# Splitting the output products of six of eight attention units into three rounded products

## The chip, the cores and the metric

One core of a Trainium2 chip. The time is the device time of the one core, in microseconds (us). An instruction queue each for TensorE (PE; its weight loads are shown as PEld), VectorE (DVE), ScalarE (ACT), GpSimd (POOL) and SyncE (SP, which here only starts transfers); each queue works strictly in order, and the queues wait for one another through semaphores.

## The reference, cut to what matters

Four batches of 512 rows of 128 numbers go through a layer norm, an attention with 16 heads of 64 and one shared key and value head, a projection back, a second norm, and a mixture of eight experts with two chosen per row:

```python
xn = _layernorm(x, ln1_g, ln1_b)
q = xn @ Wq;  k, v = split(xn @ Wkv)
attn = softmax((q * SCALE) @ k.T)
out = attn @ v                                   # 16 heads side by side: 1024 wide
x = x + _layernorm(out @ Wo, ln2_g, ln2_b)
gu = x_normed @ gate_up_w.T                      # for each expert, rows routed to it
x = x + combine(down_w @ (up * gelu(gate)))
```

The change is about `out @ Wo`. It is computed transposed: for each of the 8 pairs of heads of a batch (k counts them over all batches, 0 to 31) a 128x128 piece of Wo times the pair's 128x512 normalised attention output, summed over the 8 pairs in one bank of PSUM, `y_ps`.

## The kernel before, in words

**Units and slots.** The attention runs over 8 units, each half of a batch: 8 heads, that is 4 pairs. `attention_schedule` (L28 to L96) writes the order of all work by hand: a unit has 32 slots, one for each block of 128 keys of a head, and every step has a slot and, within it, a rank. All five engines walk the same sorted list of steps and do their own part of each. In a slot TensorE computes one 128x512 block of scores (EXP: two matmuls, L1298 and L1300, with operands rounded to fp32r), and one block for the row maxima of a later head (MAX, L1278, one matmul of fp32r); ScalarE takes the exponential (L1203), VectorE the maximum (L1123). In 4 of each 8 slots TensorE also multiplies probabilities and values (PV, L1314, in fp32). After each head (every fourth slot) GpSimd adds up its probabilities in two instructions (`fold` L1049, `psums` L1055), and for each pair it copies q (`q_hm`, L1029). Steps SUM, SUMS, SPREAD, RECIP, GATHER make the reciprocals of the softmax sums.

**Normalising and projecting a pair.** Unit u is normalised and projected while unit u+1 runs; this text calls the 32 slots of unit n stretch n, so stretch 4 holds the work on the pairs of unit 3. For pair c of a unit (0 to 3):
- NORM: TensorE spreads the reciprocals over a bank (`sum_ps`, L861, one fp32r matmul) once the pair before has been multiplied; VectorE multiplies into `ao`, which has two slots, taken in turn (L795).
- OUT: TensorE multiplies the piece of Wo (`wof`) with `ao` in fp32 (L871). A matmul of fp32 is two records in the trace.
- NORM of pair k waits, on VectorE, until OUT of pair k-2 has read its slot of `ao` (L794).

NORM stands in slots 14, 17, 19 and 22, OUT five slots later. The steps that a batch's second norm, its routing (CHOOSE0 to CHOOSE7, RANK, PLACE) and the tile lists (LIST0 to LIST3) need are spread over later slots (`AFTER_AT`). The routed rows of the first two batches leave by eight indirect transfers that GpSimd itself starts (SEND, L497), one every second slot from slot 5 to slot 19 of stretches 4 and 6. In stretches 2 and 4 a batch's input is prepared as well: XT (slot 17), XL on GpSimd (slot 17, L1059), K on TensorE (slot 21), which waits for XL. VectorE's MAX for the last head is in slot 9 of stretch 7, so TensorE waits for no maximum after that.

**The expert weights.** `raw_w` (128 partitions x 8 experts x 1024) lies in memory of its own and is filled by eight transfers at the V step of the last batch (L973 to L976, slot 25 of stretch 4). They are first used after the attention.

**The end of the attention.** In stretch 7 VectorE makes the routing and the list of the third batch, and sums the last head itself (L1144); SUM waits for it. The expert part follows in a second block of code.

Of the kernel before, what the change touches and what calls it, by code (L numbers as in the profile page):

```python
# [5 lines left out]
F32 = mybir.dt.float32  # L6
F32R = mybir.dt.float32r
# [5 lines left out]
P = 128  # L13
# [14 lines left out]
def attention_schedule(units):  # L28

    slots, lead = UH * JT, MAX_LEAD
    placed = []

    def place(slot, order, kind, u, a):
        placed.append((slot, order, (kind, u, a)))

    for n, kind in enumerate(IN_STEPS):

        place(FIRST_V_AT if kind in ("V", "VC") else -1000 + n, 4, kind, 0, 0)
        for b in range(1, units // 2):

            place(2 * slots * (b - 1) + IN_AT[n] + (LATER if b == 1 else 0), 4, kind, b, 0)
    for b in range(units // 2 - 1):
        at, lag = (AFTER_AT, 2) if b < units // 2 - 2 else (LATE_AFTER_AT, 0.25)
        for n, kind in enumerate(AFTER_STEPS):
            place(2 * slots * (b + 1) + at[n], 4, kind, b, 0)  # L60
        for n in range(TOP_K * JT if b < units // 2 - 2 else EARLY_SENDS):
            place(2 * slots * (b + 1) + at[AFTER_STEPS.index("PLACE")] + lag * n, 4.5, "SEND", b, n)
    for pair in range(units * UP):
        u, p = divmod(pair, UP)

        at = (-30, -11, *FIRST_Q_AT)[pair] if pair < 4 else 8 * pair - 19 - lead
        place(at, 3, "Q", u, p)
        place(at + 1, 3, "QHI", u, p)

        place(-8 if pair == 1 else at + 1, 4, "QLO", u, p)  # L70
        for jt in range(JT):
            place(8 * pair + PV_AT[jt], 2, "PV", u, p * JT + jt)
        place(8 * pair + PV_AT[-1] + 1, 1, "RAW", u, p)
    for n in range(units * slots):
        u, a = divmod(n, slots)
        place(n, 0, "EXP", u, a)
        place(n - 15 if n < 12 else (n - 12) // 2 if n < 32 else n - 16 - lead, 1, "MAX", u, a)
    for n, (head, _) in enumerate(shifts(units)):
        place(FIRST_SHIFT_AT[n] if n < 2 else JT * head - lead + 1, 3, "SHIFT", n, 0)
    for u in range(units):  # L80
        after = slots * (u + 1)
        if u < units - 1:
            place(after + SUM_AT[0], 5, "SUM", u, 0)
            place(after + SUM_AT[1], 5, "SUM", u, 1)
            for n, kind in enumerate(RECIP_STEPS):
                place(after + RECIP_AT[n], 5, kind, u, 0)
            for c in range(UP):
                place(after + NORM_AT[c], 5, "NORM", u, c)
                place(after + NORM_AT[c] + OUT_LAG, 5, "OUT", u, c)
        else:  # L90
# [17 lines left out]

PV_AT = (6, 8, 9, 11)

NORM_AT = (14, 17, 19, 22)

OUT_LAG = 5

RECIP_STEPS = ("SUMS", "SPREAD", "RECIP", "GATHER")

# [62 lines left out]
def bass_preln_mqa_moe_kernel(nc, x, ln1_g, ln1_b, wq, wkv, wo, ln2_g, ln2_b, gate_wT, gate_upT, downT,  # L179
# [32 lines left out]
    with ExitStack() as whole:  # L212
        def sb(stack, name, shape, dt=F32):
            return stack.enter_context(nc.sbuf_tensor(name, shape, dt))
# [4 lines left out]
        def sem(name):  # L219
            return whole.enter_context(nc.semaphore(name))  # L220
# [54 lines left out]
        jumps = sb(whole, "jumps", [P, 2 * E])  # L275
        second = sb(whole, "second", [P, REST])

        raw_w = sb(whole, "raw_w", [P, E * 2 * F])
        xs_early = sb(whole, "xs_early", [P, EARLY_ROWS, ROW])

        psums = sb(whole, "psums", [P, SUM_SLOTS, S])
# [466 lines left out]
        def load_rows(sp, k, dst):  # L748
# [6 lines left out]
            x_turned xnT_sb xh_ready xl_ready k_mm kh_ready kl_ready v_mm v_ready  # L755
            q_mm q_hi q_lo q_top max_mm max_done mrow_ready score_mm exp_done
            pv_mm raw_ready prob_folded head_sum sum_mm recip_done norm_mm ao_ready
            out_mm sums_copied spread_in rhl_in hs_in""".split()
        (wkv_in, wq_in, wo_in, ones_set, wkv_split, wq_split, headsel_set,
         x_turned, xnT_sb, xh_ready, xl_ready, k_mm, kh_ready, kl_ready, v_mm, v_ready,  # L760
         q_mm, q_hi, q_lo, q_top, max_mm, max_done, mrow_ready, score_mm, exp_done,
         pv_mm, raw_ready, prob_folded, head_sum, sum_mm, recip_done, norm_mm, ao_ready,
         out_mm, sums_copied, spread_in, rhl_in, hs_in) = [sem(n) for n in names]
        def vector_sums(head):


# [12 lines left out]
        def tail_vector(dve, kind, u, a):  # L779
            if kind == "RECIP":  # L780
                dve.wait_ge(spread_in, 32 * (u + 1))
                link(dve, nc.vector.reciprocal(rinv[:, :], spread[:, :]))
                if u >= 1:
                    dve.wait_ge(rhl_in, 32 * u)
                link(dve, nc.vector.tensor_copy(halves[:, 0, :], rinv[:, :]))
                nc.vector.tensor_tensor(halves[:, 1, :], rinv[:, :], halves[:, 0, :].bitcast(F32),
                                        ALU.subtract).then_inc(recip_done, 1)
            if kind == "NORM":
                k = u * UP + a
                dve.wait_ge(norm_mm, k + 1)  # L790
                dve.wait_ge(raw_ready, k + 1)

                if k >= 2:
                    dve.wait_ge(out_mm, k - 1)  # L794
                nc.vector.tensor_tensor(ao[:, k % 2, :], sum_ps[:, :], raw[:, k % RAW_SLOTS, :],  # L795
                                        ALU.mult).then_inc(ao_ready, 1)

# [19 lines left out]
        def tail_scalar(act, kind, u, a):  # L817
            if kind == "SUMS":
                act.wait_ge(sum_mm, 2 * (u + 1))
                if u >= 1:  # L820
                    act.wait_ge(spread_in, 32 * u)
                nc.scalar.activation(sums[:, :], sum_ps[:, :], ACT.Copy).then_inc(sums_copied, 1)
            if kind == "RAW":
                k = u * UP + a
                act.wait_ge(pv_mm, k + 1)
                if k >= RAW_SLOTS:

                    act.wait_ge(ao_ready, k - RAW_SLOTS + 1)
                nc.scalar.activation(raw[:, k % RAW_SLOTS, :], pv_ps[:, :], ACT.Copy).then_inc(raw_ready, 1)
            if kind == "OUT" and (u * UP + a) % PAIRS == PAIRS - 1:  # L830
                b = (u * UP + a) // PAIRS
                act.wait_ge(out_mm, PAIRS * (b + 1))
                if b >= 1:

                    act.wait_ge(y_turned, b)
                if b >= 1:

                    act.wait_ge(logit_mm, b)
                nc.scalar.activation(yT[:, :], y_ps[:, :], ACT.Copy).then_inc(y_ready, 1)

        def tail_tensor(pe, kind, u, a):

            b = u // 2
            if kind == "SUM":
# [18 lines left out]
            if kind == "OUT":  # L863
                k = u * UP + a
                c = k % PAIRS
                pe.wait_ge(ao_ready, k + 1)
                if k == 0:
                    pe.wait_ge(wo_in, 16)
                if c == 0 and b >= 1:
                    pe.wait_ge(y_ready, b)  # L870
                nc.tensor.matmul(y_ps[:, :], wof[:, c, :], ao[:, k % 2, :], start=c == 0,  # L871
                                 stop=c == PAIRS - 1).then_inc(out_mm, 1)


        last_pv = max(n for n, step in enumerate(steps) if step[0] == "PV")
        tail_steps = [step for step in steps[last_pv:] if step[0] in ("RAW", *RECIP_STEPS, "NORM", "OUT")]
        assert all(step in tail_steps or step[0] in ("PV", "SUM") for step in steps[last_pv:])
        steps = [step for step in steps if step not in tail_steps]

        with ExitStack() as att:  # L880
            q_hl = sb(att, "q_hl", [P, Q_SLOTS, S], F32R)
            q_hm = sb(att, "q_hm", [P, Q_SLOTS, S], F32R)
            xh = sb(att, "xh", [P, 2, S], F32R)
# [48 lines left out]
            def _(sp):  # L932
# [20 lines left out]
                for kind, u, a in steps:  # L953
# [18 lines left out]
                                         blank[:, :, :]).then_inc(rows_filled, 16)  # L972
                    if kind == "V" and u == NB - 1:  # L973
                        sp.wait_ge(rows_filled, 16 * FILLS)
                        for e in range(E):
                            load_gate_up(sp, e)  # L976
                sp.wait_ge(tiles_ready, 1)
                sp.wait_ge(rows_sent, 16 * TOP_K * TPB * (LB - 1))
# [4 lines left out]
            def _(pool):  # L983
# [27 lines left out]
                for kind, u, a in steps:  # L1011
# [29 lines left out]
                    if kind == "EXP" and a % JT == JT - 1:  # L1041
                        head = u * UH + a // JT
                        if not vector_sums(head):
# [8 lines left out]
                            if head >= SUM_SLOTS:  # L1052

                                pool.wait_ge(sum_mm, (head - SUM_SLOTS) // 4 + 1)
                            nc.gpsimd.tensor_tensor(psums[:, head % SUM_SLOTS, :], fold[:, 0, :], fold[:, 1, :],  # L1055
                                                    ALU.add).then_inc(head_sum, 1)
                    if kind == "XL" and u >= 1:
                        pool.wait_ge(xh_ready, u + 1)
                        nc.gpsimd.tensor_tensor(xl[:, u % 2, :], xnT[:, :], xh[:, u % 2, :].bitcast(F32),  # L1059
                                                ALU.subtract).then_inc(xl_ready, 1)  # L1060
# [149 lines left out]
            def _(pe):  # L1210
# [23 lines left out]
                for kind, u, a in steps:  # L1234
# [84 lines left out]
                    if (kind, u, a) == ("SUM", last_unit, 1):  # L1319

                        pe.wait_ge(tiles_ready, 1)
                        for k in range(OPEN):
                            load_expert(pe, k)
                    tail_tensor(pe, kind, u, a)
                    if kind in AFTER_STEPS:
                        after_tensor(pe, kind, u, q_ps)

# [1 line left out]
        with ExitStack() as moe:  # L1329


            GU, DN = 2 * F, FC * P
            wh = sb(moe, "wh", [P, E * GU], F32R)
            wl = sb(moe, "wl", [P, E * GU], F32R)
            wd = sb(moe, "wd", [P, E * DN])
# [494 lines left out]
```

## Time and profile before

| | |
|---|---|
| three runs | 603.86, 604.21 and 606.01 us, median 604.21 |
| profiled execution, its own time | 605.66 us |
| its span, first to last instruction | 603.7 us |
| busy: PE, PEld, DVE, ACT, POOL | 571.4, 326.3, 399.3, 297.8, 393.8 us |
| granted TensorE clock, mean | 0.983 |
| OUT of pairs 0 to 23 in the trace | 111.5 us (first) to 398.2 us (last) |

A row of the timeline gives start, duration, engine, line, operation and tiles, how many records were merged, and in brackets how long the engine had been idle and what released it. Matmuls are pipelined: the duration of one is longer than its turn, which is read from one start to the next.

### The profile page before, as it was taken

How to read it: one execution, taken by the hardware profiler on the slowest of the kernel's cores; microseconds unless marked ns; L12 is line 12 of the kernel's file. 1: busy time of each engine (PE TensorE's matmuls, PEld its weight loads, DVE VectorE, ACT ScalarE, POOL GpSimd, SP SyncE). 2: the span in 40 equal slices, each digit the busy share in tenths (PEclk: the TensorE clock that was granted, in tenths of full speed). 3: DMA queues.
4: the chain of work that ended last, by engine and by line, in shares of the span. 5: the costliest groups of instructions: out<-in, count | busy, mean ns of one | idle time of the engine just before them, and what ended most of it. 6: DMA issues, size and time to landing. Idle time of an engine off the chain costs nothing. (4 is left out here: it accounts for less than half of the span.)

```text
span 603.7 us, 8807 instructions
## 1 busy us (share of the span) xinstructions
PE 571.4 (95%) x2543; PEld 326.3 (54%) x2543; DVE 399.3 (66%) x875; ACT 297.8 (49%) x559; POOL 393.8 (65%) x329
## 2 busy tenths in 40 slices
PE   8799999999999999998999999899998898899992
PEld 6464455444545554444545545444443577788882
DVE  4878656657756869774567777876485458444463
ACT  3235655545636564463556445355635564355541
POOL 6448776667758866798598568949745944345332
PEclk9889999999999999998999999999998999999997
DMA  5111012010201200062000000000004410231042
GB/s 167 71 72 71 2 71 75 0 73 1 75 1 72 74 2 1 7 233 81 1 3 2 1 1 25 16 2 3 11 0 119 119 31 23 58 91 47 19 141 89
DMA packets 27805, 29.46 MB, mean 49 GB/s; under 512 B 7763, under 2 KB 19285, under 8 KB 27760
## 3 DMA queue, kind: packets, MB, share of 16 engines
q1 hardware_dynamic: 25056, 24.27, 12.5%
q0 software_dynamic: 2272, 4.24, 2.1%
q8 instruction: 23, 0.38, 0.3%
q10 hardware_dynamic: 432, 0.39, 0.2%
q14 instruction: 22, 0.18, 0.1%
HBM read 13.50 MB, written 15.32 MB: 48 GB/s over the span
## 5 line engine op out<-in xcount | busy, mean ns | idle before, releaser
L1203 ACT ACTIVATE prob<-s_ps 128x512 f32<-128x512 f32 x256 | 150.8, 599 | 183.3 <-PE s_ps L1300 180.9
L1123 DVE TENSOR_REDUCE less_max<-max_ps 128x1 fp32r<-128x512 f32 x256 | 174.0, 689 | 81.0 <-PE max_ps L1278 78.6
L1049 POOL TENSOR_TENSOR fold<-prob 128x1024 f32<-128x1024 f32 x63 | 149.6, 2375 | 88.7 <-ACT prob L1203 88.0
L1314 PE MATMUL pv_ps<-prob,v 128*64 128x512 f32 x512 | 138.5, 621 | 0.0
L1298 PE MATMUL s_ps<-q_hl,khh 128*128 128x512 f32 x256 | 117.9, 460 | 0.7 <-ACT prob L1203 0.7
L1278 PE MATMUL max_ps<-khh,q_hl 128*128 128x512 f32 x256 | 103.0, 408 | 5.4 <-DVE less_max L1123 4.8
L1300 PE MATMUL s_ps<-q_hm,kly 65*128 65x512 f32 x256 | 101.9, 398 | 0.0
L1298 PEld LDWEIGHTS s_ps<-q_hl,khh 128*128 128x128 f32 x256 | 48.6, 190 | 85.8 <-ACT prob L1203 67.1
L1055 POOL TENSOR_TENSOR psums<-fold 128x512 f32<-128x512 f32 x63 | 80.8, 1282 | 4.9
L1278 PEld LDWEIGHTS max_ps<-khh,q_hl 128*128 128x128 f32 x256 | 49.1, 192 | 23.4 <-DVE less_max L1123 11.1
L1300 PEld LDWEIGHTS s_ps<-q_hm,kly 65*128 65x128 f32 x256 | 48.8, 191 | 9.2 <-issue 3.3
L1314 PEld LDWEIGHTS pv_ps<-prob,v 128*64 128x64 f32 x512 | 25.6, 135 | 46.2 <-issue 34.3
L497 POOL DMA_INDIRECT sorted_rows<-xr,place_i x32 | 33.9, 1059 | 22.7 <-issue 10.9
L1108 DVE TENSOR_TENSOR q_hl<-q_ps,q_hl 64x512 fp32r<-64x512 f32 x64 | 44.1, 689 | 6.3 <-ACT q_hl L1185 4.9
L1531 DVE TENSOR_TENSOR ha<-up_ps,gl 128x512 f32<-128x512 f32 x39 | 26.9, 690 | 29.3 <-PE up_ps L1668 21.7
L1185 ACT ACTIVATE q_hl<-q_ps 64x512 fp32r<-64x512 f32 x64 | 37.6, 587 | 12.4 <-PE q_ps L1215 11.5
L1492 POOL DMA_INDIRECT parts<-raw,psums x22 | 21.8, 992 | 29.5 <-DVE raw L1540 24.3
L795 DVE TENSOR_TENSOR ao<-sum_ps,raw 128x512 f32<-128x512 f32 x32 | 22.1, 690 | 27.5 <-PE sum_ps L861 27.4
L1029 POOL TENSOR_SCALAR q_hm<-q_hl 64x1024 fp32r<-64x1024 f32 x32 | 33.3, 1041 | 8.0 <-ACT q_hl L1185 8.0
L871 PE MATMUL y_ps<-ao,wof 128*128 128x512 f32 x64 | 35.9, 646 | 0.0
L1605 ACT ACTIVATE ht<-q_ps 128x512 f32<-128x512 f32 x39 | 23.3, 597 | 23.5 <-PE q_ps L1677 23.5
L1690 PE MATMUL sum_ps<-wd,ht 128*128 x216 | 29.1, 278 | 4.6 <-DVE raw L1540 3.2
(252 smaller groups left out, 772.0 us busy)
## 6 DMA issues: line engine op xcount, KB each, us to landing
sorted_rows<-raw_w SPq DMA_DIRECT2D x36, 260.0 KB, 2.6
raw_w<-in_gate_upT SPq DMA_DIRECT2D x8, 512.0 KB, 8.5
wd<-in_downT SPq DMA_DIRECT2D x8, 256.0 KB, 4.1
raw_w<-parts SPq DMA_DIRECT2D x6, 256.0 KB, 3.4
psums<-sorted_rows SPq DMA_DIRECT2D x22, 65.0 KB, 1.9
x<-in_x SPq DMA_DIRECT2D x4, 256.0 KB, 4.2
xs_first<-sorted_rows SPq DMA_DIRECT2D x15, 65.0 KB, 1.8
out<-x SPq DMA_DIRECT2D x3, 256.0 KB, 2.1
```

The lines of the kernel that those rows point to most:

```text
L497: nc.gpsimd.indirect_dma_start(out=sorted_rows, out_offset=bass.IndirectOffsetOnAxis(ap=place_i[:, n, t:t + 1], axis=0), in_=xr[:, n, t, : ...
L871: nc.tensor.matmul(y_ps[:, :], wof[:, c, :], ao[:, k % 2, :], start=c == 0, stop=c == PAIRS - 1).then_inc(out_mm, 1)
L1049: nc.gpsimd.tensor_tensor(fold[:, :, :], prob[:, head % 4, 0:2, :], prob[:, head % 4, 2:4, :], ALU.add).then_inc(prob_folded, 1)
L1055: nc.gpsimd.tensor_tensor(psums[:, head % SUM_SLOTS, :], fold[:, 0, :], fold[:, 1, :], ALU.add).then_inc(head_sum, 1)
L1108: nc.vector.tensor_tensor(q_hl[DH:P, h % Q_SLOTS, :], q_ps[DH * hd:DH * hd + DH, :], q_hl[0:DH, h % Q_SLOTS, :].bitcast(F32), ALU.subtract ...
L1123: nc.vector.tensor_reduce(less_max[:, group % 2, col:col + 1], max_ps[:, k % 2, :], AX_X, ALU.max, negate=True).then_inc(max_done, 1)
L1185: nc.scalar.activation(q_hl[0:DH, (2 * k + hd) % Q_SLOTS, :], q_ps[DH * hd:DH * hd + DH, :], ACT.Copy).then_inc(q_hi, 1)
L1203: nc.scalar.activation(prob[:, head % 4, jt, :], s_ps[:, k % 2, :], ACT.Exp, scale=SCALE).then_inc(exp_done, 1)
L1278: nc.tensor.matmul(max_ps[:, k % 2, :], q_hl[:, k // JT % Q_SLOTS, it * P:(it + 1) * P], khh[:, b % 2, :], start=True, stop=True).then_inc ...
L1298: nc.tensor.matmul(s_ps[:, k % 2, :], khh[:, b % 2, keys], q_hl[:, slot, :], start=True, stop=False)
L1300: nc.tensor.matmul(s_ps[:, k % 2, :], kly[0:DH + 1, b % 2, keys], q_hm[0:DH + 1, slot, :], start=False, stop=True).then_inc(score_mm, 1)
L1314: last = nc.tensor.matmul(pv_ps[DH * hd:DH * hd + DH, :], v[:, b % 2, jt, :], prob[:, head % 4, jt, :], start=(jt == 0), stop=(jt == JT - 1))
```

## The change: what it does

For pairs 0 to 23 (units 0 to 5) OUT becomes three fp32r matmuls: high part of Wo times high part of `ao`, low times high, high times low. ScalarE makes the high part of `ao` (new step HIGH), GpSimd subtracts for the low part (LOW); both go to `hl`, which has three slots. GpSimd also splits Wo once, one 128x128 piece after each of heads 2 to 9. NORM moves to slots 14, 16, 19, 21, OUT to 21, 23, 25, 27, for all units but the last. NORM of pair k now waits for LOW of pair k-2 where that pair is split, for its OUT otherwise. `woh` and `hl` lie where the weights of experts 4 to 7 go; those four transfers are started after OUT of pair 23. Pairs 24 to 31 keep the fp32 product.

```diff
             for c in range(UP):
                 place(after + NORM_AT[c], 5, "NORM", u, c)
-                place(after + NORM_AT[c] + OUT_LAG, 5, "OUT", u, c)
+                if u < SPLIT_UNITS:
+                    place(after + HIGH_AT[c], 5, "HIGH", u, c)
+                    place(after + LOW_AT[c], 5, "LOW", u, c)
+                place(after + OUT_AT[c], 5, "OUT", u, c)
...
-NORM_AT = (14, 17, 19, 22)
-
-OUT_LAG = 5
+NORM_AT = (14, 16, 19, 21)
+
+HIGH_AT = (15, 17, 20, 22)
+
+LOW_AT = (18, 18, 22, 22)
+
+OUT_AT = (21, 23, 25, 27)
+
+HL_SLOTS = 3
+
+FIRST_WEIGHTS = 4
+
+SPLIT_UNITS = 6
...
-        raw_w = sb(whole, "raw_w", [P, E * 2 * F])
+        GU = 2 * F
+        with ExitStack() as split_units:
+
+            sb(split_units, "first_weights", [P, FIRST_WEIGHTS * GU])
+            woh = sb(split_units, "woh", [P, PAIRS, P], F32R)
+            hl = sb(split_units, "hl", [P, 2, HL_SLOTS, S], F32R)
+        raw_w = sb(whole, "raw_w", [P, E * GU])
...
                 if k >= 2:
-                    dve.wait_ge(out_mm, k - 1)
+                    if k - 2 < SPLIT_UNITS * UP:
+                        dve.wait_ge(al_ready, k - 1)
+                    else:
+                        dve.wait_ge(out_mm, k - 1)
                 nc.vector.tensor_tensor(ao[:, k % 2, :], sum_ps[:, :], raw[:, k % RAW_SLOTS, :],
                                         ALU.mult).then_inc(ao_ready, 1)
...
+            if kind == "HIGH":
+                k = u * UP + a
+                act.wait_ge(ao_ready, k + 1)
+
+                if k >= HL_SLOTS:
+                    act.wait_ge(out_mm, k - HL_SLOTS + 1)
+                nc.scalar.activation(hl[:, 0, k % HL_SLOTS, :], ao[:, k % 2, :],
+                                     ACT.Copy).then_inc(ah_ready, 1)
...
-                pe.wait_ge(ao_ready, k + 1)
...
-                nc.tensor.matmul(y_ps[:, :], wof[:, c, :], ao[:, k % 2, :], start=c == 0,
-                                 stop=c == PAIRS - 1).then_inc(out_mm, 1)
+                slot = k % HL_SLOTS
+                if u >= SPLIT_UNITS:
+                    pe.wait_ge(ao_ready, k + 1)
+                    nc.tensor.matmul(y_ps[:, :], wof[:, c, :], ao[:, k % 2, :], start=c == 0,
+                                     stop=c == PAIRS - 1).then_inc(out_mm, 1)
+                else:
+                    pe.wait_ge(wo_split, min(k, PAIRS - 1) + 1)
+                    pe.wait_ge(ah_ready, k + 1)
+                    nc.tensor.matmul(y_ps[:, :], woh[:, c, :], hl[:, 0, slot, :], start=c == 0, stop=False)
+                    nc.tensor.matmul(y_ps[:, :], wol[:, c, :], hl[:, 0, slot, :], start=False, stop=False)
+                    pe.wait_ge(al_ready, k + 1)
+                    nc.tensor.matmul(y_ps[:, :], woh[:, c, :], hl[:, 1, slot, :], start=False,
+                                     stop=c == PAIRS - 1).then_inc(out_mm, 1)
...
-                        for e in range(E):
+                        for e in range(FIRST_WEIGHTS):
+                            load_gate_up(sp, e)
+                    if (kind, u, a) == ("OUT", SPLIT_UNITS - 1, UP - 1):
+
+                        sp.wait_ge(out_mm, SPLIT_UNITS * UP)
+                        for e in range(FIRST_WEIGHTS, E):
                             load_gate_up(sp, e)
...
+                        if 2 <= head < 2 + PAIRS:
+
+                            if head == 2:
+                                pool.wait_ge(wo_in, 16)
+                            part = head - 2
+                            link_pool(pool, nc.gpsimd.tensor_scalar(woh[:, part, :], wof[:, part, :], 1.0, 1.0, ALU.mult,
+                                                                    ALU.mult))
+                            nc.gpsimd.tensor_tensor(wol[:, part, :], wof[:, part, :], woh[:, part, :].bitcast(F32),
+                                                    ALU.subtract).then_inc(wo_split, 1)
+                    if kind == "LOW":
+                        k = u * UP + a
+                        slot = k % HL_SLOTS
+                        if k >= HL_SLOTS:
+                            pool.wait_ge(out_mm, k - HL_SLOTS + 1)
+                        pool.wait_ge(ao_ready, k + 1)
+                        pool.wait_ge(ah_ready, k + 1)
+                        nc.gpsimd.tensor_tensor(hl[:, 1, slot, :], ao[:, k % 2, :], hl[:, 0, slot, :].bitcast(F32),
+                                                ALU.subtract).then_inc(al_ready, 1)
```

## Rows read from the trace of the kernel before

**Rows 1.** The page's groups: busy us, mean ns of one, idle before, releaser.
```profile
L1203 ACT ACTIVATE prob<-s_ps 128x512 f32<-128x512 f32 x256 | 150.8, 599 | 183.3 <-PE s_ps L1300 180.9
L1049 POOL TENSOR_TENSOR fold<-prob 128x1024 f32<-128x1024 f32 x63 | 149.6, 2375 | 88.7 <-ACT prob L1203 88.0
```
**Rows 2.** Windows by stretch: PE, PEld, DVE, ACT, POOL busy, clock, DMA share, GB/s.
```profile
102.00:153.00 51.00, 51.00 (x202) 24.56 (x200) 33.67 (x64) 24.98 (x46) 34.73 (x25) 1.00 0.12 44
...
260.00:317.00 57.00, 55.37 (x222) 27.34 (x221) 34.79 (x65) 29.52 (x58) 47.31 (x35) 0.97 0.23 84
...
371.00:423.00 52.00, 50.39 (x199) 23.63 (x197) 38.88 (x84) 26.19 (x50) 42.27 (x33) 1.00 0.03 9
```
**Rows 3.** Timeline of PE, stretch 1: PV, OUT, NORM, scores; then a rounded product.
```profile
114.90 1.08 PE L1314 MATMUL pv_ps<-prob,v 128*64 128x512 f32 x4
115.91 1.12 PE L871 MATMUL y_ps<-ao,wof 128*128 128x512 f32 x2
116.47 0.79 PE L861 MATMUL sum_ps<-rhl,headsel 128*128 128x512 f32 x1
117.10 0.39 PE L1298 MATMUL s_ps<-q_hl,khh 128*128 128x512 f32 x1
...
117.80 0.40 PE L1213 MATMUL q_ps<-xh,wqh 128*128 128x512 f32 x1
...
118.50 0.39 PE L1298 MATMUL s_ps<-q_hl,khh 128*128 128x512 f32 x1
```
**Rows 4.** The same of stretch 3: PV and NORM with no OUT between them.
```profile
212.79 1.08 PE L1314 MATMUL pv_ps<-prob,v 128*64 128x512 f32 x4
...
213.80 0.50 PE L861 MATMUL sum_ps<-rhl,headsel 128*128 128x512 f32 x1
214.14 0.40 PE L1298 MATMUL s_ps<-q_hl,khh 128*128 128x512 f32 x1
```
**Rows 5.** Windows of POOL alone: length, busy, instructions; between and in the SEND stretches.
```profile
253.90:281.00 27.10, 25.00 (x19) 0.94 0.49 174
370.40:392.50 22.10, 20.64 (x15) 1.00 0.06 19
220.00:253.90 33.90, 19.58 (x16) 1.00 0.01 1
```
**Rows 6.** Timeline of stretch 4, slots 19 to 23.
```profile
271.05 0.79 PE L861 MATMUL sum_ps<-rhl,headsel 128*128 128x512 f32 x1
...
273.45 1.27 POOL L1059 TENSOR_TENSOR xl<-z,xh 128x512 fp32r<-128x512 f32 x1
...
274.87 0.47 PE L1213 MATMUL q_ps<-xh,wkh 128*128 128x512 f32 x1 [1.63 <-POOL xl L1059]
274.89 0.99 POOL L497 DMA_INDIRECT sorted_rows<-xr,place_i  x1 [0.17 <-issue]
...
276.61 1.97 PE L1314 MATMUL pv_ps<-prob,v 128*64 128x512 f32 x4
```
**Rows 7.** Timeline of stretch 6, slots 19 to 23.
```profile
381.19 1.12 PE L871 MATMUL y_ps<-ao,wof 128*128 128x512 f32 x2
...
383.02 0.97 POOL L497 DMA_INDIRECT sorted_rows<-xr,place_i  x1 [0.30 <-issue]
...
384.21 2.28 DVE L655 TENSOR_TENSOR cmp<-more,tri 128x64 f32<-128x64 f32 x1
...
388.21 1.29 DVE L1123 TENSOR_REDUCE less_max<-max_ps 128x1 fp32r<-128x512 f32 x2
...
388.95 0.50 PE L1278 MATMUL max_ps<-khh,q_hl 128*128 128x512 f32 x1 [1.53 <-DVE less_max L1123]
```
**Rows 8.** Timeline of stretch 7: the unsplit pairs, and the end of the attention.
```profile
432.80 1.13 PE L871 MATMUL y_ps<-ao,wof 128*128 128x512 f32 x2
...
434.25 0.69 DVE L795 TENSOR_TENSOR ao<-sum_ps,raw 128x512 f32<-128x512 f32 x1 [1.42 <-PE sum_ps L861]
...
444.19 0.22 DVE L655 TENSOR_TENSOR cmp<-more,tri 128x64 f32<-128x64 f32 x1
...
455.33 1.06 PE L851 MATMUL sum_ps<-psums,sumsel 128*32 128x512 f32 x8 [1.37 <-DVE psums L1144]
```
**Rows 9.** Timeline of POOL at the start: splitting a 128x256 piece of another weight.
```profile
10.30 0.41 POOL L990 TENSOR_SCALAR wqh<-prob 128x256 fp32r<-128x256 f32 x1
10.79 1.09 POOL L991 TENSOR_TENSOR wql<-prob,wqh 128x256 fp32r<-128x256 f32 x1
```

More of the change, by code:

```diff
@@ L276, in bass_preln_mqa_moe_kernel @@
         second = sb(whole, "second", [P, REST])
-        raw_w = sb(whole, "raw_w", [P, E * 2 * F])
+        GU = 2 * F
[4 more added lines that the diff above has]
+        raw_w = sb(whole, "raw_w", [P, E * GU])
+        assert PAIRS * P + 2 * HL_SLOTS * S == (E - FIRST_WEIGHTS) * GU
         xs_early = sb(whole, "xs_early", [P, EARLY_ROWS, ROW])
@@ L757, in bass_preln_mqa_moe_kernel @@
             pv_mm raw_ready prob_folded head_sum sum_mm recip_done norm_mm ao_ready
-            out_mm sums_copied spread_in rhl_in hs_in""".split()
+            out_mm sums_copied spread_in rhl_in hs_in ah_ready al_ready wo_split""".split()
         (wkv_in, wq_in, wo_in, ones_set, wkv_split, wq_split, headsel_set,
@@ L762, in bass_preln_mqa_moe_kernel @@
          pv_mm, raw_ready, prob_folded, head_sum, sum_mm, recip_done, norm_mm, ao_ready,
-         out_mm, sums_copied, spread_in, rhl_in, hs_in) = [sem(n) for n in names]
+         out_mm, sums_copied, spread_in, rhl_in, hs_in, ah_ready, al_ready, wo_split) = [sem(n) for n in names]
         def vector_sums(head):
@@ L839, in tail_scalar, with tail_tensor @@
                 nc.scalar.activation(yT[:, :], y_ps[:, :], ACT.Copy).then_inc(y_ready, 1)
-        def tail_tensor(pe, kind, u, a):
+        def tail_tensor(pe, kind, u, a, wol=None):
             b = u // 2
@@ L870, in tail_tensor @@
                     pe.wait_ge(y_ready, b)
-                nc.tensor.matmul(y_ps[:, :], wof[:, c, :], ao[:, k % 2, :], start=c == 0,
-                                 stop=c == PAIRS - 1).then_inc(out_mm, 1)
+                slot = k % HL_SLOTS
[11 more added lines that the diff above has]
+                                     stop=c == PAIRS - 1).then_inc(out_mm, 1)
         last_pv = max(n for n, step in enumerate(steps) if step[0] == "PV")
-        tail_steps = [step for step in steps[last_pv:] if step[0] in ("RAW", *RECIP_STEPS, "NORM", "OUT")]
+        tail_steps = [step for step in steps[last_pv:] if step[0] in ("RAW", *RECIP_STEPS, "NORM", "HIGH", "LOW", "OUT")]
         assert all(step in tail_steps or step[0] in ("PV", "SUM") for step in steps[last_pv:])
@@ L880, in bass_preln_mqa_moe_kernel @@
         with ExitStack() as att:
+            wol = sb(att, "wol", [P, PAIRS, P], F32R)
             q_hl = sb(att, "q_hl", [P, Q_SLOTS, S], F32R)
@@ L1323, in _ @@
                             load_expert(pe, k)
-                    tail_tensor(pe, kind, u, a)
+                    tail_tensor(pe, kind, u, a, wol)
                     if kind in AFTER_STEPS:
@@ L1329, in bass_preln_mqa_moe_kernel @@
         with ExitStack() as moe:
-            GU, DN = 2 * F, FC * P
+            DN = FC * P
             wh = sb(moe, "wh", [P, E * GU], F32R)
```

## The prediction

> **What bounds the kernel now.** I read the windows by stretch first. In stretch 1 TensorE is busy for all 51.00 us of 51.00, in stretch 4 for 55.37 of 57.00, in stretch 6 for 50.39 of 52.00, while ScalarE and VectorE have a quarter or more of each stretch free and GpSimd is at 34.73 of 51, 47.31 of 57 and 42.27 of 52 us [rows 2]. So through the attention every instruction taken from TensorE shortens the run by its turn, and every wait of TensorE lengthens it. The page's groups say the same: the exponentials and the folds had 183.3 and 88.7 us of idle time ahead of them, nearly all spent on what TensorE drives [rows 1].
>
> Then I looked at GpSimd alone, because it has the highest load beside TensorE. In the middle of stretch 4 it is busy 25.00 of 27.10 us, in stretch 6 20.64 of 22.10, but only 19.58 of 33.90 between [rows 5]. What is missing in the first two windows are gaps of some 0.2 to 0.3 us around the indirect transfers (0.17 and 0.30 in the rows), so there GpSimd has no time left. Both places show in TensorE: K waits 1.63 us for GpSimd's XL, and behind that wait the PV group at 276.61 takes 1.97 us where another takes 1.08: the mean granted clock of that window is 0.94, so a few us of it ran at the lower level, 1.2 GHz [rows 3, 5, 6]. In stretch 6 a MAX waits 1.53 us for VectorE, whose list step has an instruction of 2.28 us beside a fold, where the same one takes 0.22 us in stretch 7 [rows 7, 8].
>
> **What goes, on TensorE.** With OUT between PV and NORM, from the start of PV to the scores after it are 117.10 - 114.90 = 2.20 us; with NORM alone 214.14 - 212.79 = 1.35 us. One OUT in fp32 costs 0.85 us [rows 3, 4]. A rounded product of three fp32r matmuls takes 118.50 - 117.80 = 0.70 us [rows 3], the same shapes and type as the new one. That is 0.15 to 0.16 us less for each of 24, **3.8 us** in all, and the most this change can give through TensorE. Its bounds: 24 x 0.34 = 8 us if the three overlapped so well that each cost 0.17, to a loss of 24 x (3 x 0.34 - 0.85) = 4 us if each of them came as slowly as the scores behind a fp32 product (214.14 - 213.80 = 0.34 us) [rows 4]; I take 0.70, since its own row shows it.
> The Trainium skill (FP8 and Floating Point Precision, section TensorE Precision Notes) says that true FP32 is four passes through the array. By that alone three passes would save a quarter of 0.85, 0.21 us each or 5.1 us. The trace speaks for 3.8.
>
> **What is added and hidden.** HIGH is a 128x512 activation, 0.60 us as the exponentials [rows 1]: 24 of them, 14.4 us, on an engine idle for half of each stretch. I cost them at nothing: HIGH of the first pair runs right behind its exponential, in the gap before the next scores are there. If that cover were gone each would push an exponential by up to 0.6 us, which TensorE notices only two blocks later. Splitting Wo is 8 pieces of at most half the 128x256 pair of 0.41 and 1.09 us, so up to 8 x 1.5 = 12 us even unhalved, over 50 us in which GpSimd is idle for a third: nothing on the path [rows 2, 9]. On SP the four late transfers stand behind OUT of pair 23, near 399 us; their first reader comes only behind the last SUM of the attention at 455.33 [rows 8], when TensorE waits for all eight, so over 50 us of delay cost nothing. The earlier four leave the queue sooner; as nothing waited for them, no gain.
>
> **LOW is what is not hidden.** It is a GpSimd subtraction of 128x512, as XL is: 1.27 us [rows 6]. Four per stretch are 5.1 us. In stretch 1 GpSimd has 16 us free, and 14 in the 33.9 us before the transfers of stretch 4 [rows 2, 5]; stretches 1, 2, 3 and 5 have no such transfers, and there I take it that LOW of pair 0 is done by the time that NORM of pair 2 wants its slot of `ao`. From the order of steps, NORM of pair 2 (slot 19) now waits on VectorE for LOW of pair 0 (slot 18); behind it queue all later maxima, and on TensorE OUT of pair 0 and NORM of pair 3 (slot 21) wait for the same LOW. TensorE's NORM of pair 2 takes the place where OUT stood. TensorE has two blocks (2 x 0.70) and OUT ahead of NORM of pair 3; VectorE needs 0.7 us for its multiplication and about 0.1 for the handing over. So LOW may end up to 1.5 us after NORM of pair 2 starts. This is the point from which it decides.
> - Stretch 4. GpSimd ends XL at 274.72 and the transfer of slot 17 at 275.88, so LOW ends at 277.2. NORM of pair 2 starts at about 270.6, the start of OUT before. LOW is 5 us past the point. TensorE waits for XL at K as before (now from 272.2), ends K at 275.6, waits in OUT to 277.3 and in NORM to 278.0, then maxima and the low part of k run late on VectorE. By counting turns the scores of slot 24 start at 282.9, and did at 281.6 before; as two cheaper OUTs (0.3 us) are in this, the wait costs 1.6 us. The lower clock cost some 1.4 us before (1.97 - 1.08 for PV, as much relatively for OUT behind it); with twice the idle time I take one more such piece, 1.5 us. **+3.1 us**, with bounds of 0 (all absorbed) and 5.
> - Stretch 6. The transfer of slot 17 ends at 383.99, LOW at 385.3, against 381.3 for NORM of pair 2 [rows 7]. VectorE's multiplication ends at 386.1. Only then does it take the next maximum and LIST0, which took 4.3 us (383.9 to 388.2), because two of its instructions sat out a fold and a sum; the fold is pushed back by the two LOWs and meets it again. Its next maximum ends at 391.6, so the MAX on TensorE that started at 388.95 starts at 391.7. Before it OUT of pair 1 was already done, now it comes after: +0.7. The scores of slot 24 start 3.5 us later; without the two savings inside, **+3.8 us**. Bounds 1 (the list step meets no fold) and 7 (two pieces at the lower clock).
> - Stretch 7. Pair 26 may not overwrite `ao` until OUT of pair 24 has read it, and that OUT has moved from slot 19 (before NORM) to 21 (behind it). So VectorE waits for two score blocks and an OUT: 2 x 0.47 + 0.1 + 0.85 us from NORM on, and NORM of pair 27 on TensorE waits 0.8 for the multiplication behind it. Slots 21 and 23 have no PV beside them, so each fp32 OUT there costs a change of type and back, 0.2 us. VectorE's list chain is as late, and TensorE's last SUM waits for it already (1.37 us) [rows 8]. **+1.6 us**, bounds 0.5 and 3.
>
> Sum: -3.8 + 3.1 + 3.8 + 1.6 = **+4.7 us**. The profiled execution took 605.66 us, 1.96 over its span; it would be 610.4. It lies 1.45 over the median of the runs, so against the median of 604.21 the forecast is **608.8 us**.
>
> **Rivals.**
> 1. *LOW is there in time* (not slower). If VectorE's wait costs nothing, because GpSimd reaches LOW within 1.5 us of NORM, the gain of 3.8 stays and only stretch 7 pays: 604.2 - 3.8 + 1.6 = 602.0, or 600.4 if that is hidden too. For it: a third of GpSimd's time in stretch 1 is idle. Against it: in stretches 4 and 6 it is the order of its own queue, not speed elsewhere, that puts LOW behind two transfers, and these windows have none to give.
> 2. *The waits are half as long*: TensorE meets them with work that I have put after them, or the lower clock stays away. Stretches 4 and 6 then cost 3.3 together: 604.2 - 3.8 + 3.3 + 1.6 = 605.3.
> 3. *VectorE becomes the bound by the shared memory path.* The 2.28 us against 0.22 shows that a small VectorE instruction can sit out a GpSimd one. Routing steps of stretches 3 and 5 and lists of 6 and 7 stand in slots 20 to 31, next to LOW. Four more MAX waits of 1.5 us like that of stretch 6 make 608.8 + 6 = 615. Against: in stretches 3 and 5 LOW ends before the routing's instructions with two memory operands begin. The Trainium skill (SBUF — State Buffer, section SBUF: two separate sides) says that GpSimd and a VectorE instruction with two SBUF inputs take the pair of ports as a lock for the whole instruction. By it the maxima and multiplications, which read PSUM, don't suffer, and each LOW may hold up a list instruction.
> 4. *Change without effect*: the weights' memory or Wo's split could stall the start; no row has anything waiting there.
>
> **How the numbers follow.** About 0.5%, 3.0 us, can be told from no change. Forecast 0.52, own range 607.2 to 611.5. Rival 1 0.13: half of it below 601.2. Rival 2 with rival 4 0.25, between 603 and 607. Rival 3 0.10, above 611.5. So faster 0.07, same 0.31 (0.06 + 0.25), slower 0.62. The range leaves out the faster tail and half of rival 3: 602.0 to 612.5.
>
> **What would show it.** Right: PE waits named after VectorE's multiplication or LOW in stretches 4 and 6, LOW of pair 12 ending some 5 us after NORM of pair 14 starts; a later `ao` multiplication of pair 26 than of the OUT of 24; stretches 1, 2, 3 and 5 shorter by about 0.6 us each. Wrong: GpSimd taking LOW before the transfers, or TensorE's stretches 4 and 6 as long as before. A clock below 0.983 over the span would say that the lower level cost more than I took.

## The result, and the profile after

The changed kernel takes 612.00 us (median of 4 runs, 611.81 to 612.21), the kernel before, on the same chip, 604.04 us (603.81 to 606.01): ratio 1.0125, 95% interval 1.0104 to 1.0147. It is slower by 8.0 us. The forecast was 608.8 us and slower; the direction is right, the size is 3.2 us short. The measured time lies inside the stated range of 602.0 to 612.5 us but 0.5 us above the narrower range given to the mechanism forecast, 607.2 to 611.5.

The profiled execution of the changed kernel took 611.81 us, 609.7 of it span, at a mean clock of 0.978 (before: 605.66, 603.7 and 0.983). From its page: the load of the engines, and the two groups of [rows 1] as they are now.

```profile
PE 572.4 (94%) x2567; PEld 330.6 (54%) x2567; DVE 398.4 (65%) x875; ACT 311.6 (51%) x583; POOL 430.3 (71%) x369
L1268 ACT ACTIVATE prob<-s_ps 128x512 f32<-128x512 f32 x256 | 151.1, 599 | 161.8 <-PE s_ps L1365 158.4
L1096 POOL TENSOR_TENSOR fold<-prob 128x1024 f32<-128x1024 f32 x63 | 149.9, 2380 | 56.4 <-ACT prob L1268 55.6
```

GpSimd has 36.5 us more work (430.3 against 393.8) and ScalarE 13.8; the folds still cost 150 us but have 32 us less free time ahead of them. TensorE's busy time rose by a microsecond although 24 products became cheaper; some 27 us of its span ran at the lower clock, some 20 in the first profile of before.

The windows of [rows 2] again. Their bounds are not those of the stretches: in the trace before, stretch 1 runs from 79.9 to 132.4 us, stretch 4 from 239.3 to 297.4, stretch 6 from 350.3 to 404.3, so each window goes from about slot 14 of its stretch to slot 14 of the next. In the first of them TensorE is still never idle, in the other two its busy time fell (55.37 to 53.39, and 50.39 to 49.07 us) and the granted clock with it (0.97 to 0.94, and 1.00 to 0.97).

```profile
102.00:153.00 51.00, 51.00 (x207) 25.48 (x208) 34.00 (x65) 27.71 (x52) 40.16 (x29) 1.00 0.12 44
...
260.00:317.00 57.00, 53.39 (x216) 27.50 (x214) 31.41 (x58) 29.79 (x58) 49.77 (x37) 0.94 0.14 45
...
371.00:423.00 52.00, 49.07 (x193) 24.00 (x191) 37.61 (x78) 27.03 (x50) 44.09 (x34) 0.97 0.15 51
```

To say where the time went I took, from both traces, the start of the score block at a given slot, counted from the first score block of the attention. "1.00" is slot 0 of stretch 1; a number is the kernel named minus the first profile of before, in us (negative: ahead). "End" is the end of the last instruction. The other columns are kernels described below. Four of them (e1, e6, e7, e8) had no spell at half clock between 30 and 35 us, where the other six profiles had one, and are 0.8 to 0.9 us ahead in every line from there on; e8 is the kernel before itself, so this is no effect of a change in the code.

```
slot        after    e1     e2     e3     e4     e5     e6     e7     e8
0.08         0.0   -0.9   +0.1    0.0    0.0    0.0   -0.8   -0.9   -0.8
2.00        -0.5   -1.3    0.0   -0.5   -0.5   -0.5   -1.5   -1.5   -0.8
4.00        -1.2   -2.0    0.0   -1.2   -1.2   -1.1   -2.5   -2.5   -0.8
4.16        -1.2   -2.0    0.0   -1.2   -1.1   -1.1   -2.5   -2.5   -0.8
4.24        +2.3   -5.8   -3.4   +2.4   +0.7   -2.7   -6.2   -6.2   -2.4
6.16        +1.9   -5.9   -3.4   +1.9   +0.3   -2.8   -6.6   -6.7   -2.3
6.24        +5.0   -6.4   -5.2   +5.1   +3.1   -2.8   -7.0   -7.2   -2.4
7.00        +4.8   -6.5   -5.2   +5.0   +2.9   -2.8   -7.4   -6.2   -2.4
7.16        +4.8   -5.4   -4.2   +5.0   +2.9   -2.8   -6.2   -6.2   -2.4
last SUM    +5.9   -4.3   -3.1   +5.0   +4.0   -2.8   -5.1   -5.2   -2.3
end         +6.2   -0.7   -2.2   +7.9   +5.3   -2.0   -3.8   -3.4   -0.2
```

In column "after", stretches 1, 2, 3 and 5 gain 0.45, 0.56, 0.19 and 0.16 us; stretch 4 loses 3.3, stretch 6 3.0, stretch 7 1.1, the expert part 0.3.

The timeline of stretch 4 shows how. It answers to [rows 6].

```profile
270.98 1.07 POOL L517 DMA_INDIRECT sorted_rows<-xr,place_i  x1 [0.17 <-issue]
272.08 1.27 POOL L1124 TENSOR_TENSOR xl<-z,xh 128x512 fp32r<-128x512 f32 x1
273.49 0.47 PE L1278 MATMUL q_ps<-xh,wkh 128*128 128x512 f32 x1 [2.52 <-POOL xl L1124]
273.51 0.99 POOL L517 DMA_INDIRECT sorted_rows<-xr,place_i  x1 [0.17 <-issue]
274.53 2.51 POOL L1120 TENSOR_TENSOR hl<-ao,hl 128x512 fp32r<-128x512 f32 x2
275.87 0.79 PE L912 MATMUL y_ps<-hl,woh 128*128 128x512 f32 x1 [0.96 <-POOL hl L1120]
275.94 0.69 DVE L818 TENSOR_TENSOR ao<-sum_ps,raw 128x512 f32<-128x512 f32 x1 [7.07 <-POOL hl L1120]
278.75 1.98 PE L1379 MATMUL pv_ps<-prob,v 128*64 128x512 f32 x4
```

Read it from GpSimd's rows: transfer, XL, transfer, and only then the two LOWs. VectorE stood still for 7.07 us in front of its multiplication, TensorE 2.52 us for XL (1.63 before) and 0.96 for LOW in the middle of an OUT, and 3 us later a PV group takes 1.98 us: half clock. This spell lasted 6.8 us, the one of before 3.4. XL itself did not come later: it started 1.4 us earlier than in [rows 6], as far as everything else was ahead at slot 16. TensorE reached K another 0.9 us sooner, since an OUT (0.85 us) that stood ahead of K now stands behind it; that is why the wait at K grew.

Stretch 6, which answers to [rows 7]:

```profile
384.69 0.97 POOL L517 DMA_INDIRECT sorted_rows<-xr,place_i  x1 [0.30 <-issue]
385.68 2.51 POOL L1120 TENSOR_TENSOR hl<-ao,hl 128x512 fp32r<-128x512 f32 x2
387.01 0.49 PE L912 MATMUL y_ps<-hl,woh 128*128 128x512 f32 x1 [1.77 <-POOL hl L1120]
387.09 0.69 DVE L818 TENSOR_TENSOR ao<-sum_ps,raw 128x512 f32<-128x512 f32 x1 [4.44 <-POOL hl L1120]
387.93 0.47 PE L892 MATMUL sum_ps<-rhl,headsel 128*128 128x512 f32 x1 [0.42 <-DVE ao L818]
388.13 2.37 POOL L1096 TENSOR_TENSOR fold<-prob 128x1024 f32<-128x1024 f32 x1
388.61 1.99 DVE L675 TENSOR_TENSOR cmp<-more,tri 128x64 f32<-128x64 f32 x1
389.50 1.98 PE L1379 MATMUL pv_ps<-prob,v 128*64 128x512 f32 x4
393.05 0.50 PE L1343 MATMUL max_ps<-khh,q_hl 128*128 128x512 f32 x1 [0.73 <-DVE less_max L1188]
```

TensorE waits 1.77 + 0.42 + 0.73 = 2.92 us where it waited 1.53 before, and here too a spell of 3.4 us at half clock follows that before did not have.

And stretch 7, for [rows 8]: VectorE now waits for OUT's product, TensorE for VectorE's multiplication; the last SUM waits as before (1.36 us).

```profile
438.71 1.02 PE L904 MATMUL y_ps<-ao,wof 128*128 128x512 f32 x2
439.87 0.69 DVE L818 TENSOR_TENSOR ao<-sum_ps,raw 128x512 f32<-128x512 f32 x1 [2.79 <-PE y_ps L904]
440.70 0.47 PE L892 MATMUL sum_ps<-rhl,headsel 128*128 128x512 f32 x1 [0.97 <-DVE ao L818]
...
461.04 1.06 PE L882 MATMUL sum_ps<-psums,sumsel 128*32 128x512 f32 x8 [1.36 <-DVE psums L1209]
```

### The profile page after: what moved, and what is told of

It reads as the page before. It is cut to its first block and busy times, and to the rows that moved or that the text cites. A ratio compares the mean times of both kernels' runs of the same rounds, so it can differ in the third digit from the quotient of the medians.

```text
span 609.7 us, 8983 instructions
## 1 busy us (share of the span) xinstructions
PE 572.4 (94%) x2567; PEld 330.6 (54%) x2567; DVE 398.4 (65%) x875; ACT 311.6 (51%) x583; POOL 430.3 (71%) x369
## 5 line engine op out<-in xcount | busy, mean ns | idle before, releaser
L1363 PE MATMUL s_ps<-q_hl,khh 128*128 128x512 f32 x256 | 115.2, 450 | 0.4 <-ACT prob L1268 0.4
L1662 ACT ACTIVATE gl<-gate_ps 128x512 f32<-128x512 f32 x39 | 23.3, 598 | 19.1 <-PE gate_ps L1733 16.0
```

The lines of the kernel that those rows point to most:

```text
L1363: nc.tensor.matmul(s_ps[:, k % 2, :], khh[:, b % 2, keys], q_hl[:, slot, :], start=True, stop=False)
```

## The experiments

The first four ran on one chip, the last four on a second. The kernel before took 605.9 us on the one (603.9 to 608.8, 22 runs) and 605.5 us on the other (603.8 to 608.0, 18 runs). It scatters more there than beside the result, so ratios are compared and not times.

**e1: the changed kernel with the transfers out of the way.** Of the eight transfers of a row block in stretches 4 and 6, the last five move from slots 11 to 19 to slots 23 to 31.

```diff
-            place(2 * slots * (b + 1) + at[AFTER_STEPS.index("PLACE")] + lag * n, 4.5, "SEND", b, n)
+            late = 6 if b < units // 2 - 2 and n >= 3 else 0
+            place(2 * slots * (b + 1) + at[AFTER_STEPS.index("PLACE")] + lag * (n + late), 4.5, "SEND", b, n)
```

> The changed kernel with five of the eight indirect transfers of stretches 4 and 6 (slots 11 to 19) moved to slots 23 to 31, so that neither XL nor LOW stands behind them. Theory A (LOW is late because GpSimd's own queue is full there): LOW of pairs 12 and 20 ends some 5 us earlier, VectorE's waits for it (7.07 and 4.44 us in the changed kernel) go below 1 us, so do K's wait (2.5 us) and OUT's (0.96 and 1.77 us), and no lower clock in the two stretches: 602 to 604 us against 612.0. Theory B (HIGH and LOW cost by their mere number, through shared memory paths and busier engines): 610 us or more, wherever the transfers stand.

Measured: 602.55 us (12 runs), ratio 0.9942 (0.9923 to 0.9960). The 1.2% lost became 0.6% won. In the timeline of stretch 4, XL, LOWs and K:

```profile
266.77 1.27 POOL L1125 TENSOR_TENSOR xl<-z,xh 128x512 fp32r<-128x512 f32 x1
268.00 2.55 POOL L1121 TENSOR_TENSOR hl<-ao,hl 128x512 fp32r<-128x512 f32 x2
269.15 0.39 PE L1279 MATMUL q_ps<-xh,wkh 128*128 128x512 f32 x1
270.32 0.40 PE L913 MATMUL y_ps<-hl,woh 128*128 128x512 f32 x1
271.59 1.08 PE L1380 MATMUL pv_ps<-prob,v 128*64 128x512 f32 x4
```

XL and the LOWs come 5.3 and 6.5 us earlier than in the changed kernel (1.7 us of it because all of e1 is that far ahead by slot 16), K and OUT carry no wait, and PV runs at full clock. Nothing was made cheaper; GpSimd's work was put in another order. Together with e2 below that settles the cause: not the 24 LOWs as such, but XL and LOWs queued behind transfers that nobody was waiting for. With the transfers in their old places the change costs 1.25%; with the transfers moved on both sides the two ratios are 0.9942 with the products and 0.9955 without.

**e2: the same move in the kernel before.** The same edit of one line, without the three products.

> The kernel before with the same five transfers moved to slots 23 to 31, nothing else. Theory A: K's wait for XL (1.6 us) goes, and the spell at the lower clock behind it: 601 to 602.6 against 604.0. If the transfers cost as much in their new place: 604.

Measured: 602.80 us (11 runs), ratio 0.9955 (0.9938 to 0.9973). So most of e1's gain over before is not the products' but belongs to a fault that the kernel before had already. Its K waited 1.63 us for XL, and its MAX in stretch 6 waited 1.53 us for a list step beside a fold [rows 6, 7]; here neither waits, and that list instruction takes a seventh of the time:

```profile
379.64 0.33 DVE L656 TENSOR_TENSOR cmp<-more,tri 128x64 f32<-128x64 f32 x1
```

The two intervals overlap, so the runs don't tell whether the three products are worth anything here; by the slot table, without the 0.9 us by which e1 was ahead from slot 8 on, e1 ends the attention 3.4 us ahead of before and e2 3.1.

**e3: the unsplit units at the slots of before.** Units 6 and 7 get NORM at 14, 17, 19, 22 and OUT five slots later again.

```diff
+                if not (u < SPLIT_UNITS):
+                    place(after + OLD_NORM_AT[c], 5, "NORM", u, c)
+                    place(after + OLD_NORM_AT[c] + 5, 5, "OUT", u, c)
+                    continue
...
```

> The changed kernel with NORM and OUT of the unsplit units at their old slots (NORM 14, 17, 19, 22, OUT five later), all else as changed. Theory A: stretch 7 gives back what it lost, 1.1 us from the trace of the changed kernel (1.6 in the prediction): 610.9. Rival: the end of the attention hangs on VectorE's list chain anyway: 612.

Measured: 612.01 us (6 runs), ratio 1.0088 (1.0060 to 1.0116). The last SUM comes 0.9 us sooner than in the changed kernel (+5.0 against +5.9), all of it in stretch 7. The times don't resolve that: the intervals of the two ratios overlap, and this profile lost another 2.9 us in the expert part, with two spells at half clock there.

**e4: four `ao` slots for the split units.** NORM of a pair then waits for the LOW four pairs back and not two, so VectorE does not stand still. To find room, the gate and up weights of the first four experts are loaded with the others, at OUT of pair 23.

```diff
-                if k >= 2:
-                    if k - 2 < SPLIT_UNITS * UP:
-                        dve.wait_ge(al_ready, k - 1)
...
+                if k < SPLIT_UNITS * UP:
+                    if k >= 4:
+                        dve.wait_ge(al_ready, k - 3)
...
```

> The changed kernel with four slots of ao for the split pairs (in memory of experts 1 and 2, so that all eight weight transfers start after OUT of pair 23): NORM of a pair waits for LOW of the fourth pair back, not the second. OUT still waits for LOW on TensorE. Theory A1 (most of the cost is VectorE standing still in NORM, and the list and maxima late behind it): 606 to 608. Theory A2 (most is TensorE's own wait for XL and in OUT): 609 to 611. Rival: moving all weight transfers costs, over 612.

Measured: 612.56 us (6 runs), ratio 1.0116 (1.0083 to 1.0148). VectorE's longest wait is gone, and hardly any time with it. TensorE's waits for GpSimd's products stayed:

```profile
274.56 0.76 PE L1281 MATMUL q_ps<-xh,wkh 128*128 128x512 f32 x1 [2.51 <-POOL xl L1127]
...
275.60 2.51 POOL L1123 TENSOR_TENSOR hl<-ao_split,hl 128x512 fp32r<-128x512 f32 x2
...
386.43 0.80 PE L917 MATMUL y_ps<-hl,woh 128*128 128x512 f32 x1 [1.81 <-POOL hl L1123]
```

The last SUM is 1.9 us nearer to before's (+4.0), 1.7 of it in stretch 4. There the OUT no longer waits, but the matmuls ahead of it ran at half clock, from K on, which hides a wait as well. How much of the 1.7 us is VectorE's and how much is where the spell fell stays open. The 7.07 us of VectorE, the most striking number in the trace, decide at most a third of the loss (1.9 of 5.9 us), and the run times show none of it. The later weight transfers are part of this kernel too; its expert part is 1.3 us longer than in the first profile, which is within the scatter told at the end, so what they cost alone was not tested.

**e5: split only where there are no transfers.** Units 3 and 5, whose products fall into stretches 4 and 6, keep one fp32 product and the old slots, as do 6 and 7.

```diff
+                if not (u in SPLIT):
+                    place(after + OLD_NORM_AT[c], 5, "NORM", u, c)
...
+SPLIT = (0, 1, 2, 4)
...
```

> The changed kernel, but units 3 and 5 (whose NORM and OUT fall into the crowded stretches 4 and 6) keep their one fp32 product and the slots of before, as does unit 6; only units 0, 1, 2 and 4 are split (16 products). Theory A (the cost is GpSimd's full queue in stretches 4 and 6, elsewhere each split product saves what the changed kernel's trace shows): stretches 4 and 6 end as far behind before as they begin, stretches 1, 2, 3 and 5 give 0.45, 0.56, 0.19 and 0.16 us, and the last SUM stands 1.3 to 1.5 us ahead of before's: 602.6 us against 604.0, ratio 0.998. Theory B (a split unit costs time wherever it stands, by what its LOW takes from folds and its type changes from TensorE): the last SUM stands behind before's and the ratio is over 1.000. If a split product saved the 0.16 us of my prediction without loss, 16 would give 2.6 us, ratio 0.996.

Measured: 604.01 us (12 runs, one of them 610.3), ratio 0.9978 (0.9953 to 1.0004), so the time can't be told from before's. In the trace stretch 6 now costs nothing. Up to stretch 4 the gain is the changed kernel's; in stretch 4 itself it is 1.5 us more than expected, which e8 explains.

**e6: everything together.** e1's transfers, e3's slots, and the third OUT of a split unit at slot 25.5, where it stands behind SUM and ahead of fp32r scores, and no longer between PV and SUM, which are both fp32.

```diff
-OUT_AT = (21, 23, 25, 27)
+OUT_AT = (21, 23, 25.5, 27)
```

> The changed kernel with the five later transfers of each row block moved behind the LOWs (as in e1), unit 6 at the slots of before, and the third OUT of each split unit at slot 25.5, behind the SUM of slot 25, so that it no longer stands between two fp32 neighbours of that slot. Theory A: the pieces add up. From the slot table of e1 (last SUM 4.3 us ahead of before) comes another 0.9 for unit 6's slots (e3) and up to 0.15 us for each of six third products: last SUM 5 to 6 us ahead of before's, ratio 0.989 to 0.992, about 1.3 us below e1's. Rival: the slots that the stretches win are lost again in stretch 7 behind the transfers moved into it (e1 lost 1.1 us in its slots 8 to 16), and in the expert part, which waits for something of its own: ratio as e1's, 0.994.

Measured: 601.12 us (6 runs), ratio 0.9937 (0.9911 to 0.9962). The lowest of all by number, but its interval covers the ratios of e1, e2 and e7, and the 1.3 us under e1 that I expected are not there. The new slot is worth 0.19, 0.08, 0.21 and 0.14 us in stretches 1, 2, 3 and 5 against e1, which has the same transfers; from 1.24 to 2.00 this kernel gains 0.33 us and the changed kernel 0.15. Stretch 7 gave 1.2 us back in its slots 8 to 16, where TensorE waits 1.02 us for the rows of the second norm (`xr`) at 418.86 us, and the last SUM waits longer for VectorE's sums (2.28 us, 1.37 before [rows 8]):

```profile
449.54 1.07 PE L888 MATMUL sum_ps<-psums,sumsel 128*32 128x512 f32 x8 [2.28 <-DVE psums L1215]
```

**e7: e6 with the last three transfers 1, 1.5 and 2 slots earlier.**

```diff
-            late = 6 if b < units // 2 - 2 and n >= 3 else 0
+            late = (6, 6, 5.5, 5.25, 5)[n - 3] if b < units // 2 - 2 and n >= 3 else 0
```

> As e6_all_three, but the last three of the five moved transfers stand 1, 1.5 and 2 slots earlier, so that the last is at slot 29 and not at 31, and GpSimd's work on the next block's rows (the z and x products, and the mean and rstd behind them) is not pushed back. Theory A: the 1.0 us that e1 and e2 lose in slots 8 to 16 of stretch 7 comes from there; the last SUM is 0.5 to 1.0 us ahead of e6's, ratio 0.001 to 0.002 lower. Rival: that 1.0 us has another cause (the products of GpSimd there wait for ScalarE's exps), and the time is e6's, within 0.3 us.

Measured: 601.25 us (7 runs), ratio 0.9938 (0.9915 to 0.9960): e6's time. The 1.2 us of stretch 7 are gone and reappear between slot 24 of stretch 6 and stretch 7. I expected a gain and there is none. With a third transfer ahead of it, a fold starts at 391.60 us and not at 390.38, a list instruction of VectorE takes 1.49 us and not 0.23 beside it, and a MAX on TensorE waits:

```profile
391.60 2.40 POOL L1102 TENSOR_TENSOR fold<-prob 128x1024 f32<-128x1024 f32 x1
392.61 1.49 DVE L697 TENSOR_TENSOR passed<-passed,more 128x72 f32<-128x72 f32 x1
396.37 0.50 PE L1349 MATMUL max_ps<-khh,q_hl 128*128 128x512 f32 x1 [1.02 <-DVE less_max L1194]
```

So the earlier transfer picked another victim.

**e8: the kernel before once more**, for a second profile.

> The kernel before once more, with one blank added in a line and nothing else changed, for a second profile of it: does the chain of its expert part lose time to lower-clock spells in one execution and not in another? Theory A (before's own profile, 605.66 us, lay above its median of 604.0): the slots of the attention part agree with the first profile within 0.1 us, and the distance from last SUM to end differs by 0.5 to 3.7 us. Rival: the expert part repeats within 0.2 us, and the spells seen in e1's and e3's expert parts are those kernels' own.

One run, 605.10 us, span 603.1. Its attention is not the same as in the first profile: in stretch 4 it gains 1.56 us (the column steps from -0.8 to -2.4). The rows of that place:

```profile
273.73 0.47 PE L1213 MATMUL q_ps<-xh,wkh 128*128 128x512 f32 x1 [1.64 <-POOL xl L1059]
...
275.29 1.08 PE L1314 MATMUL pv_ps<-prob,v 128*64 128x512 f32 x4
```

The wait is the same, 1.64 us against 1.63 [rows 6], but PV takes 1.08 us and not 1.97: no spell followed. So one spell of 3.4 us costs 1.56 us here, and the same wait brings it on in one execution and not in another (e5, with a wait of 1.66, had none either). In exchange this execution lost 2.1 us in the expert part, where it had a spell at 514 us and the first profile had none (that one had a spell at 457 us, where the expert part begins). My expectation that the attention part repeats to 0.1 us fell; the one on the expert part held.

## Why the prediction was right in sign and short in size

- **The product's price: right where it stood among its like, too high on the whole.** I took 0.15 to 0.16 us for each of 24. The first two of a stretch give just that (0.31 us by slot 24 of stretch 1). The other two give 0.15 us together, because the new slot 25 lies between PV and SUM, both fp32, and the change of type costs what the product saves; e6 confirms it by moving that one OUT half a slot. Stretches 3 and 5 gave 0.3 to 0.4 us less than stretches 1 and 2. Of that, 0.17 and 0.18 us are a wait of TensorE for a maximum in slot 31, which grew from 0.17 to 0.34 us in stretch 3 and from 0.24 to 0.42 in stretch 5; the rest was not followed up. Over stretches 1, 2, 3 and 5: 2.5 us forecast, 1.4 seen. I had charged two changes of type in stretch 7 and forgotten them everywhere else.
- **Stretch 4: right in mechanism.** LOW of pair 12 ended at 275.8 us, 6.7 us after NORM of pair 14 started on TensorE (269.08); the waits at K (2.6 forecast, 2.52 seen) and in OUT are those named. Net of the four savings of the stretch I forecast 2.5 us and saw 3.3. e1 shows the cause.
- **Stretch 6: right size, partly by another way.** Forecast 3.2 net, seen 3.0. I had a MAX waiting for a delayed list step: the list step did sit out a fold again, L675 ending with it (1.99 us; 2.28 before, 0.22 undisturbed [rows 7, 8]), but the MAX waited only 0.73 us. The time went into OUT's and NORM's waits (2.2 us) and 3.4 us of half clock, which I had only as an upper bound. The Trainium skill (SBUF — State Buffer, section SBUF: two separate sides) says that of a GpSimd instruction that reads SBUF and a VectorE instruction with two SBUF inputs the one that starts first keeps the shared ports until it is done, and the other is blocked. The trace agrees: L675 has two operands in SBUF, started at 388.61 us inside the fold (388.13 to 390.50) and ended at 390.60.
- **Stretch 7: right in mechanism, 0.5 us too much.** 1.6 forecast, 1.1 seen, and e3 gets 0.9 of it back with the old slots.
- **VectorE's standing still** was in my account the head of the chain. e4 removes it and leaves the slowness: the waits that count are TensorE's own, for XL and LOW.
- **The step that failed: from the profile to the median.** It is half of the 3.2 us. The terms gave +4.7 us against the profiled execution, and the profiles differ by 6.15: 1.45 short, which is about the product's price (1.1), stretch 4 (0.8) and the expert part (0.3), less what I had too much for stretches 6 and 7 (0.2 and 0.5). I then took another 1.45 us off (and 604.21 + 4.7 is 608.9, not 608.8), since before's profiled execution lay that much over its median. But that execution had a spell after a wait of 1.6 us, which e8 and e5 did not have, and its price of 1.56 us is about the 1.62 us between 605.66 and the median of 604.04. The changed kernel waits longer, and the three profiles that have its waits (its own, e3's, e4's) all show 6.8 us of half clock in stretch 4 and 3.4 in stretch 6; it lies at its own median (611.81 against 612.00). If before's faster executions lack that spell, then against their median both spells in full are new. 6.15 + 1.62 + 0.19 is the 8.0 measured, but that sum comes out whatever the 1.62 us consist of. That the faster executions lacked the spell is inferred from the match of 1.56 and 1.62 and from e8 and e5, not seen in their own traces, and the match can be chance: e8 without the spell took 605.10 us, and the first profile had other spells too, at 30 us (worth 0.8) and at 457 us. What speaks for spells in general is the granted clock: of the 40 runs of before beside the experiments the nine under 604.8 us all had 0.988 to 0.993, the first profile 0.983. I had named one sign of this miss beforehand, a mean clock below 0.983; it was 0.978.

The rivals: LOW in time fails in stretches 4 and 6 and holds in 1, 2, 3 and 5, where TensorE never waits for LOW (VectorE once, 2.14 us); half the waits fails; the shared path costs the one list step, as before, and its four further MAX waits of 1.5 us did not come. So 612.00 us lies in the band above 611.5 that I had given to that rival, but by the forecast mechanism; that the time still fell inside the whole range is in part luck. The change did have an effect, and nothing waited on Wo's split or on the late weights.

## What to carry to other kernels

An engine that is 65% busy can still have no room in the two windows where it matters, so read its windows stretch by stretch, and before you give it work that the bounding engine waits for, move what nobody waits for (here five transfers) behind it: that was worth 0.5% in the kernel before, and with the change in it took the kernel from 1.2% slower to 0.6% faster, no clear part of which is the change's own. Price a cheaper product together with its neighbours: a change of number type on both sides ate the whole gain of 0.15 us at one place of the four in a stretch. And when the profile of before lies above its median, look for the event that makes it so, and ask whether the change makes that event certain, before taking the difference off.

## What the runs showed that I had not expected

- The lower clock is a matter of chance at waits of about 1.6 us and was there each time at 2.5 us: after 1.63 to 1.66 us of waiting in stretch 4 one of three profiles had a spell (before, not e5 and e8), after 2.5 us all three (the changed kernel, e3 and e4). In stretch 6 waits of 1.48 to 1.53 us brought none in three profiles (before, e5 and e8), and 1.77 to 1.81 us in an OUT one in each of three. In the expert part waits of 1.76 to 1.99 us were followed by a spell in five profiles of eight. A spell of 3.4 us cost 1.56 us in stretch 4.
- The expert part repeats less well than the attention. Its duration differed from the first profile's by +0.3 (changed kernel), +0.8 (e5), +0.9 (e2), +1.3 (e4, e6), +1.8 (e7), +2.1 (e8), +2.9 (e3) and +3.7 us (e1). Six of these nine profiles show a spell between 495 and 523 us; e7 has none and loses 1.8 us all the same. One place sets the two shortest expert parts apart: behind VectorE's list of the last block, TensorE waited 1.32 us in the first profile and in the changed kernel, and 1.76 to 1.99 us in the eight others, among them e8, which is the same kernel as the first.

```profile
513.95 1.15 PE L1690 MATMUL sum_ps<-wd,ht 128*128 x8 [1.32 <-DVE raw L1540]
...
512.22 1.15 PE L1690 MATMUL sum_ps<-wd,ht 128*128 x8 [1.76 <-DVE raw L1540]
```

The first row is the first profile's, the second e8's. This scatter is as large as what e1 to e7 differ by in the end, so the attention was judged by its last SUM; what sets it was not tested.
